# A routed low-rank feed-forward block on one core: the first weight chunk's cast split over two engines, one load on another queue, and another order of the last matmuls

## What is computed

```python
y   = x @ W + (x @ lora_A[idx[b]]) @ lora_B[idx[b]]        # per sequence b, rank 16
out = x + y @ W_base.T + b_base
          + sum_e route_w[e] * (y @ A[e].T) @ B[e].T       # 8 experts, rank 16
# route_w: softmax of y @ W_gate.T, top 2 of 8, renormalised
```

## Time and profile before

| | |
|---|---|
| median of 3 runs | 66.01 us |
| lowest, highest | 65.82, 66.3 us |
| the profiled execution | 66.16 us |
| its span | 65.0 us |
| TensorE, VectorE, ScalarE, GpSimd busy | 60.7, 37.6, 25.9, 17.0 us |

### The profile page before, as it was taken

One profiled execution on the slowest core, in us unless ns is written; L12 is line 12 of the kernel. 1 busy time (PEld: TensorE's weight loads), 2 busy tenths in 40 slices (PEclk: granted clock), 3 DMA queues, 4 the chain that ended last, 5 costly groups with the idle time before them and its releaser, 6 DMA issues.

```text
span 65.0 us, 1269 instructions
## 1 busy us (share of the span) xinstructions
PE 60.7 (93%) x420; PEld 59.7 (92%) x420; DVE 37.6 (58%) x130; ACT 25.9 (40%) x73; POOL 17.0 (26%) x41
## 2 busy tenths in 40 slices
PE   4995999999999999999999999999999999999940
PEld 4994999999999999999999999999999999998920
DVE  0946469789979837020787758980487140486120
ACT  4433598655194470001162436511371011361340
POOL 1005998999884002130020301130000000000000
PEclk9999999999999999999999999999999999999999
DMA  0799999915886001332323322810025000035026
GB/s 0 206 287 295 329 373 399 358 35 153 304 275 257 5 0 34 69 66 62 69 59 77 66 46 61 299 49 0 0 101 222 0 10 0 0 113 209 0 86 237
DMA packets 5048, 8.46 MB, mean 130 GB/s; under 512 B 1057, under 2 KB 1569, under 8 KB 5042
## 3 DMA queue, kind: packets, MB, share of 16 engines
q1 hardware_dynamic: 4514, 7.70, 37.5%
q0 software_dynamic: 384, 0.56, 2.3%
q10 hardware_dynamic: 144, 0.13, 0.6%
HBM read 5.26 MB, written 2.10 MB: 113 GB/s over the span
## 4 chain that ended last, share of the span: by engine, by line
PE 87%; DMA 5%; SPq 1%; ACT 1%; DVE 1%; issue 0%
PE bank L477 22%; PE bank L479 21%; PE bank L478 21%; PE bank L485 9%; PE bank L487 7%; DMA w_raw<-fold_in 5%; PE bank L528 2%; PE bank L544 2%; PE bank L534 1%; ACT wg_hi L273 1%; PE bank L518 1%; DVE y_out L473 1%; SPq L180 1%; SPq L179 1%; PE bank L564 0%
## 5 line engine op out<-in xcount | busy, mean ns | idle before, releaser
L477 PE MATMUL bank<-cl_hi,x_hi 128*128 128x408 f32 x32 | 11.4, 356 | 0.0
L479 PE MATMUL bank<-cl_hi,x_lo 128*128 128x408 f32 x32 | 11.1, 348 | 0.0
L478 PE MATMUL bank<-cl_lo,x_hi 128*128 128x408 f32 x32 | 11.1, 348 | 0.0
L477 PE MATMUL bank<-cr_hi,x_hi 128*128 128x256 f32 x32 | 9.7, 303 | 0.0
L478 PE MATMUL bank<-cr_lo,x_hi 128*128 128x256 f32 x32 | 9.0, 282 | 0.0
L479 PE MATMUL bank<-cr_hi,x_lo 128*128 128x256 f32 x32 | 9.0, 281 | 0.0
L260 POOL CAST cl_hi<-lora_raw 128x64 fp32r<-128x64 f32 x8 | 1.9, 238 | 19.2 <-PE bank L479 19.1
L439 DVE MAX8 top_val<-bank 128x8 f32<-128x8 f32 x8 | 1.4, 169 | 8.6 <-PE bank L528 8.6
L477 PEld LDWEIGHTS bank<-cr_hi,x_hi 128*128 128x128 f32 x32 | 6.1, 190 | 0.1
L477 PEld LDWEIGHTS bank<-cl_hi,x_hi 128*128 128x128 f32 x32 | 6.0, 188 | 0.1
L478 PEld LDWEIGHTS bank<-cr_lo,x_hi 128*128 128x128 f32 x32 | 6.1, 190 | 0.0
(11 more groups left out here) (97 smaller groups left out, 154.7 us busy)
## 6 DMA issues: line engine op xcount, KB each, us to landing
x_raw<-x_t SPq DMA_DIRECT2D x8, 256.0 KB, 4.8
out<-y_out SPq DMA_DIRECT2D x7, 256.0 KB, 2.1
w_raw<-fold_in SPq DMA_DIRECT2D x4, 256.0 KB, 5.4
w_raw<-fold_in SPq DMA_DIRECT2D x3, 324.0 KB, 5.4
bw_rows<-bw_hi SPq DMA_DIRECT2D x16, 40.5 KB, 2.0
lora_raw<-lora POOLq DMA_DIRECT2D x8, 64.0 KB, 4.8
bw_rows<-bw_lo SPq DMA_DIRECT2D x8, 40.5 KB, 2.0
ffn_b_raw<-ffn_b SPq DMA_DIRECT2D x1, 256.0 KB, 7.5
```

The costliest lines, as they stand in the source:

```text
L477: nc.tensor.matmul(out, a_hi, b_hi, start=first, stop=False, skip_group_check=True)
L478: nc.tensor.matmul(out, a_hi, b_lo, start=False, stop=False, skip_group_check=True)
L479: return nc.tensor.matmul(out, a_lo, b_hi, start=False, stop=last, skip_group_check=True)
```

## The change

Four edits, in three places of the program:

- W_base's first chunk is cast by two engines: VectorE casts its left 256 columns (a new instruction ahead of all its low parts, with a semaphore of its own), ScalarE the right 256. TensorE's first 8 matmuls of chunk 0 are sorted: four on the left columns, then four on the right.
- The first weight piece is issued by ScalarE, ahead of its table load, and no more by SyncE.
- At the end tile 6's `Lora_right` goes ahead of tile 7's transpose and its `Delta` right behind it, both ahead of tile 7's last two right chunks. `Last_delta` is gone; tile 7 ends with the ordinary `Delta`, three matmuls for the left half and then three for the right.
- The last two copies change engines: VectorE copies tile 7's left half, stored by SyncE; ScalarE the right half, stored from its own queue.

```diff
@@ sync_program
-            sp.dma_start(w_raw[:, 0, FIRST:D + GH], fold_in[0, :, FIRST:D + GH]).then_inc(w_first_loaded, DMA)
             sp.dma_start(w_raw[:, 0, 0:FIRST], fold_in[0, :, 0:FIRST]).then_inc(wa_loaded[0], DMA)
...
-            sp.wait_ge(last_right_copied, 1)
-            sp.dma_start(out[NT - 1, :, HALF:], y_out[:, NT - 1, HALF:]).then_inc(out_stored, DMA)
+            sp.wait_ge(last_left_copied, 1)
+            sp.dma_start(out[NT - 1, :, 0:HALF], y_out[:, NT - 1, 0:HALF]).then_inc(out_stored, DMA)
@@ scalar_program
+            act.dma_start(w_raw[:, 0, FIRST:D + GH], fold_in[0, :, FIRST:D + GH]).then_inc(w_first_loaded, DMA)
             nc.scalar.activation(table_warm[:], nc.const_aps.tensor(0.0, [P, 1], F32), ACT.Exp)
...
                 act.wait_ge(wb_loaded[m], DMA)
-                nc.scalar.copy(wg_hi[:, m, wg_cols(m)], raw_wg(m)).then_inc(w_hi_done, 1)
+                if m == 0:
+
+                    nc.scalar.copy(wg_hi[:, 0, LEFT:], w_raw[:, 0, D + LEFT:]).then_inc(w_hi_done, 1)
+                else:
+                    nc.scalar.copy(wg_hi[:, m, :], raw_wg(m)).then_inc(w_hi_done, 1)
...
-            copy_left(NT - 1)
-            act.wait_ge(yl_done, NT)
-            act.dma_start(out[NT - 1, :, 0:HALF], y_out[:, NT - 1, 0:HALF]).then_inc(out_stored, DMA)
+            copy_right(NT - 1)
+            act.wait_ge(yr_done, NT)
+            act.dma_start(out[NT - 1, :, HALF:], y_out[:, NT - 1, HALF:]).then_inc(out_stored, DMA)
@@ vector_program
+            dve.wait_ge(wb_loaded[0], DMA)
+            nc.vector.tensor_copy(wg_hi[:, 0, GH:LEFT], w_raw[:, 0, D + GH:D + LEFT]).then_inc(wb_left_hi_done, 1)
+            dve.wait_ge(wb_left_hi_done, 1)
...
-            dve.wait_ge(zr_done, NT)
-            nc.vector.tensor_copy(y_out[:, NT - 1, HALF:], right(NT - 1)).then_inc(last_right_copied, 1)
+
+            dve.wait_ge(zl_done, NT)
+            nc.vector.tensor_copy(y_out[:, NT - 1, 0:HALF], left(NT - 1)[:, OUT_LEFT]).then_inc(last_left_copied, 1)
@@ tensor_program
-            def Lora_right(q):
-                for t in (2 * q, 2 * q + 1):
+            def Lora_right(q, tiles):
+                for t in tiles:
...
             for m in range(KC - 1):
-                pe.wait_ge(w_hi_done, 2 * m + 2)
-                fold_pass(m, wt_hi, wg_hi)
+                if m == 0:
+                    pe.wait_ge(w_hi_done, 1)
+                    pe.wait_ge(wb_left_hi_done, 1)
+                    for i in range(KC):
+                        nc.tensor.matmul(bank[i][:, GH:LEFT], wt_hi[:, 0, i * P:(i + 1) * P], wg_hi[:, 0, GH:LEFT],
+                                         start=False, stop=False, skip_group_check=True)
+                    pe.wait_ge(w_hi_done, 2)
+                    for i in range(KC):
+                        nc.tensor.matmul(fold_right(i), wt_hi[:, 0, i * P:(i + 1) * P], wg_hi[:, 0, LEFT:],
+                                         start=(i % 2 == 0), stop=False, skip_group_check=True)
+                else:
+                    pe.wait_ge(w_hi_done, 2 * m + 2)
+                    fold_pass(m, wt_hi, wg_hi)
...
             T2(t)
             Right(t + 1, (0, 1))
+            Lora_right(PAIRS - 1, (t,))
             T2(t + 1)
+            Delta(t)
             Right(t + 1, (2, 3))
-            Lora_right(PAIRS - 1)
-            Delta(t)
-            Last_delta()
+            Lora_right(PAIRS - 1, (t + 1,))
+            Delta(t + 1)
```

More of the change, by code:

```diff
@@ L105, in adaln_ffn_kernel @@
         bwl_bank, bwr_bank = bank[6], bank[7]
-        w_first_loaded = sem("w_first_loaded")
+        w_first_loaded, wb_left_hi_done = sem("w_first_loaded"), sem("wb_left_hi_done")
         wa_loaded = [sem(f"wa_loaded{m}") for m in range(KC)]
@@ L122, in adaln_ffn_kernel @@
         bw_summed, bw_hi_done, bw_lo_done = sem("bw_summed"), sem("bw_hi_done"), sem("bw_lo_done")
-        last_right_copied = sem("last_right_copied")
+        last_left_copied = sem("last_left_copied")
         even_zeros, odd_zeros = sem("even_zeros"), sem("odd_zeros")
@@ L487, in fold_pass @@
                     nc.tensor.matmul(fold_right(i), w[:, m, rows], wg[:, m, LEFT:],
-                                     start=(m == 0 and w is wt_hi and wg is wg_hi and i % 2 == 0), stop=False, skip_group_check=True)
+                                     start=False, stop=False, skip_group_check=True)
             def Left(t, chunks):
@@ L553, in Delta @@
                         False, True).then_inc(zr_done, 1)
[L555 to L564, removed]
             ones = nc.const_aps.tensor(1.0, [P, P], mybir.dt.bfloat16)
@@ L610, in tensor_program @@
             Lora_left(0)
-            Lora_right(0)
+            Lora_right(0, (0, 1))
             Left(2, ALL)
@@ L629, in tensor_program @@
                 Lora_left(q)
-                Lora_right(q - 1)
+                Lora_right(q - 1, (t - 2, t - 1))
                 Delta(t - 2)
```

## The result

Six runs of each kernel, taken in turn on one chip: the changed kernel has a median of 65.31 us (64.95 to 65.6), the one before 65.99 us (65.7 to 66.56). The ratio is 0.9867 with a 95% interval of 0.983 to 0.9905, so by the interval the change saves 0.63 to 1.12 us; the two medians themselves differ by 0.68. The profiled execution took 65.07 us with a span of 63.9, against 66.16 and 65.0 before. Single executions of 67.5 us and more occur with several of these kernels, the one before among them; ratios leave them out.

What follows compares the result with a forecast made beforehand. TensorE, ending the chain for 87% of the span, was taken as the bound. Start 0.15, matmul 0.12, copy 0.05 and landing 0.40 sum to 0.72 us: 66.16 to 65.44 profiled, 65.3 against the median; range 64.9 to 65.9.

Steps and rivals of the forecast that it cites:

- The landing: End of the kernel: with tile 6's store sent earlier, the last store lands 1.7 us after issue, not 2.1; 0.40 us saved.
- A floor of 2.0 us: Rival, last store: a landing never takes less than 2.0 us, so the gain is 0.42 and the time 65.6; chance 0.25.
- The last matmul: Tail: 19 matmuls in place of 20 behind the second transpose, so the last one starts 0.12 us earlier.
- the copy: Tail: ScalarE copies the last right half and issues its store sooner after the last matmul than VectorE and SyncE; 0.05 us.
- The cast split: Start: chunk 0's left matmuls start 0.20 us earlier, but chunk 1's cast still ends at 8.59; worth nothing by itself.
- Its price on VectorE: Start: VectorE's cast of 256 columns of W_base's first chunk, taken as 0.42 us from a same-size copy out of PSUM.
- The first piece's move: Start: SyncE's other issues move up 0.44 us, of which unused DMA engine time lets 0.15 us come through.
- What bounds the start: Start: TensorE's own chain and chunk 1's load and cast end within 0.05 us of each other at 8.64.
- one of its signs of being right: Start: a new TensorE wait of about 0.2 us before chunk 1, ended by ScalarE's cast, which ended with its load.
- The forecast for chunk 1: Start: TensorE starts chunk 1's matmuls at 8.49 in place of 8.64.
- The late piece as a rival: Start: ScalarE's issue served late delays TensorE; lateness beyond 0.7 us costs time, giving 66.6 or 66.9 us; chance 0.05.
- Its sign of a clock below 1.00: Start: a granted clock below 1.00 in chunk 0 would show the prediction wrong; at 1.2 GHz, 28 matmuls cost some 3 us more.

Runs made afterwards that it cites:

- the order alone: Kernel before with only the new order of the last matmuls, copies and stores unexchanged; one profile, 68.03 us, 55.7 us from chunk 1's first matmul to the end.
- the copies alone: Kernel before with only the last two copies and their stores exchanged, matmuls in the old order; one profile, 56.2 us from chunk 1's first matmul to the end.
- the split alone: Kernel before with only W_base's first cast split over two engines and chunk 0's first 8 matmuls sorted; ratio 0.997 to the kernel before.
- small-load profile: Changed kernel with SyncE issuing the 2 KB bias load first, ahead of its weight pieces; profile 67.5 us, ratio 0.993 to the kernel before.
- split and tail: Changed kernel with its first weight piece issued by SyncE again; ratio 0.993 to the kernel before.
- tail only: Kernel before with only the new order of the last matmuls and the exchanged last copies and stores; ratio 0.997 to the kernel before.

## Why the prediction was right, and where its sizes were off

The forecast was 65.3 us; 65.31 was measured, inside the range. That it came so near is in part luck. The sum was made for the profiled execution, from 66.16 to 65.44, and that one came out at 65.07: the two profiles differ by 1.1 us and not by 0.72. Point by point:

- *The landing* (0.40). Right in its mechanism, a little large: 0.3 us, from 2.1 to 1.8. The bytes moved on their own, as the order alone and the copies alone show between them. A floor of 2.0 us did not appear: 1.7 and 1.8 were measured. The fixed part of about 2.0 us plus the bytes, which the Trainium skill gives for transfers that GpSimd issues (DMA: Bandwidth & Descriptors, section "Anatomy of one DMA"), does not describe these stores of SyncE and ScalarE.
- *The last matmul* (0.12) and *the copy* (0.05). Right. From chunk 1's first matmul to the last matmul's start it is 62.11 - 8.64 = 53.47 before and 61.32 - 8.04 = 53.28 after: 0.19, of which the one matmul is 0.12. From the last matmul's start to the last issue it is 0.77 before and 0.72 after. All together 0.5 in the profiles in place of 0.57; the timed runs give the tail 0.3, with 0.2 of uncertainty.
- *The cast split* worth nothing by itself. The mechanism was right and is shown by the 0.61 us wait with the split alone; the timed runs leave room for 0.2 us. Its price on VectorE was 0.29 us, below the 0.42 that was taken. Taken out of the changed kernel, it changed nothing that could be measured.
- *The first piece's move* (0.15). This is the step that was mis-sized, and for a wrong reason. The prediction had held that "what they can regain is unused engine time: (1 - 0.60) x 0.45 = 0.18 us", since the engines were "full" after 2.90. A share of 1.09 at 296 GB/s was no ceiling: with two queues started together the share was 1.02 and the rate 332 GB/s, or 1.06 and 365. Nor were the engines full all the time after 2.90: from 5.00 to 6.00, which the prediction did not look at, the share before was 0.79. And the gain is not in the first stretch: the second profile of the changed kernel moved only 108 GB/s there, against 131 before. Leaving out the order-only and the small-load profile, chunk 1's cast ended at 7.85 to 8.75 in five profiles with one queue and at 7.29 to 7.89 in seven with two. So it ended some 0.7 us earlier (means 7.61 and 8.31), not 0.15. W_base's first chunk, too, was there by 4.3 to 4.5 in all seven, and at 4.6 to 5.3 in the five; in copies only its lateness alone (5.30) put chunk 1 at 8.90. Why two queues move more is open.
- *What bounds the start.* The prediction had TensorE's chain start at the old 3.42 and then wait 0.2 us for chunk 1, which was one of its signs of being right. It started at 3.75 and 3.90, and waited for no load after that. The prediction named the sharing of engines in one sentence beside the Trainium skill's rule and did not carry it into the sum. The first piece was 0.3 to 0.5 us late by it, which cost part of what the early loads gave. The rule's other half, that a second queue saves only issuing time, does not fit the rates above. In the profiles chunk 1 starts on average at 8.16 with two queues (seven) and at 8.62 with one (five): 0.45 us, three times the 0.15, and the timed pairs give 0.4. The forecast for chunk 1 was 8.49. The changed kernel's two profiles had 8.04 and 8.50, and the second agrees only because its raw matmuls were slow.
- *The late piece as a rival* was the right mechanism in small: late by 0.3 to 0.5. The prediction called 0.7 us free, reckoning with a load that holds TensorE until 8.64. With chunk 1's cast done some 0.7 us earlier none of it was free. Its sign of a clock below 1.00 could not have warned: the granted clock read 1.00 even while matmuls started 0.21 us apart in place of 0.12 (last section).

By the timed pairs the start (queue and split together) gave about 0.6 us in place of 0.15, and the tail 0.3 in place of 0.57. Errors of opposite sign went into the sum, and that is the luck in it. The scatter of the runs adds to it: the changed kernel had a ratio of 0.987 here and of 0.991, 0.6 us, in another session.

## What to carry to other kernels

A wait that one edit removes can be the second of two that end together: look for what ends next before counting the gain. When three small edits come together, time them in all combinations and average the pairs; single pairs put the same edit here at anything from 0.1 to 0.6 us. If the last store lands slowly, ask what was sent just ahead of it: finishing the last tile but one early took 0.3 us off a 2.1 us landing with no work removed. A full DMA share is no proof of a full rate, and a piece moved to a second queue to run beside others will itself land later.

## What the runs showed of the hardware that was not expected

**TensorE's first matmuls run at a pace that turns at a different moment in each execution.** The eight records of the raw matmuls in two kernels with the same code up to there (min/median/max in ns), split and tail, then tail only:

```profile
L571 PE MATMUL bank<-w_raw x8: 434/434/537, 3.4 to 5.2; 128*128 128x136 f32 x8
```

```profile
L564 PE MATMUL bank<-w_raw x8: 279/279/430, 3.4 to 4.5; 128*128 128x136 f32 x8
```

In the one all eight were slow, in the other all but the first were fast, so that they took 2.18 us against 1.38. That is as much as the whole change is worth and part of why single profiles can't weigh a start. The granted clock reads 1.00 in both, so which of the two levels (1.2 and 2.4 GHz) it was is not shown by that column, only the pace. The Trainium skill (TensorE: Matmul & The Clock Gate, section "Part 1: The HAM clock gate") says that half rate is the default state, that activity releases it, and that the moment differs from run to run; the paces agree, and no granted clock here shows it.

**After a pause early on the slow pace can last.** In the order-only execution W_base's first chunk landed only at 5.95. TensorE's timeline:

```profile
6.62 0.58 PE L485 MATMUL bank<-wg_hi,wt_hi 128*128 128x256 f32 x1 [1.04 <-ACT wg_hi L273]
...
9.57 0.41 PE L487 MATMUL bank<-wg_hi,wt_lo 128*128 128x256 f32 x1
9.78 0.36 PE L485 MATMUL bank<-wg_hi,wt_lo 128*128 128x256 f32 x1
9.97 0.28 PE L487 MATMUL bank<-wg_hi,wt_lo 128*128 128x256 f32 x1
```

After raw matmuls that had all been slow and a pause of 1.04 us, matmuls started 0.21 us apart until 9.8, and 0.12 apart from then on; the granted clock read 1.00 in both. Chunk 0 took 4.44 us (6.62 to 11.06) in place of 2.92, and the execution 68.03. The small-load profile (67.5 us) has the same picture, with a pause of 0.43 and fast matmuls from 9.7. Copies only had a pause of 1.07 us after raw matmuls that had already turned fast, and took no harm. That would say that late loads hurt most when the turn has not yet come; with three cases that is argued, not shown. It fits that of the 54 timed executions with two weight pieces started together none took 67 us, while 7 of 113 with one queue did, the kernel before included, and 3 of 13 with the small load ahead.

**GpSimd's first transfer comes later when the two queues start together.** It issued its first LoRA load at 5.5 to 5.6 in the six profiles whose weight pieces start on SyncE alone and in the one with the small load ahead, and at 6.7 to 7.4 in the seven with two pieces started together. Why, and why the loads of all later pieces are faster then, stays open. It is not the LoRA traffic alone: in 2.90 to 5.00 none of it is issued yet in any profile, and the rates already are 296 and 332 GB/s.
